# Counting the adjacency in groups of four chunks that share one PSUM bank

## The reference

```
x = x + relational layer(h): segment_sum of norm * (h @ weight[etype])[src] over dst
x = x + two gcn_conv layers(h): out = A_norm @ (h @ W) + b
x = x + equivariant message layer(h): messages of 128-node features, edge filters, segment_sum over src
x = x + two sage_conv layers(h): (segment_sum(x[src], dst) / deg) @ W_l.T + x @ W_r.T + b
```

## Time and profile before

| | us |
|---|---|
| median of 3 runs | 2048.51 |
| lowest, highest | 2046.33, 2052.84 |
| span of the profiled execution | 1473.0 |
| median less span | 575.5 |
| from the first to the last count | 209.3 |
| TensorE busy, share of the span | 93% |
| VectorE, ACT, POOL busy, share of the span | 59%, 34%, 60% |

### The profile page before, as it was taken

The page is one execution under the profiler, slowest core; times in us unless marked ns, Lnnn a source line. Parts: engine busy times, 40 slices in busy tenths (PEclk is TensorE's granted clock), DMA queues, the critical chain, the costliest instruction groups (busy, mean ns, idle before and its releaser), DMA issues.

```text
span 1473.0 us, 24743 instructions
## 1 busy us (share of the span) xinstructions
PE 1374.9 (93%) x6924; PEld 931.9 (63%) x6925; DVE 868.2 (59%) x2488; ACT 494.3 (34%) x1269; POOL 886.3 (60%) x930
## 2 busy tenths in 40 slices
PE   4887899999999999999999978999999979999998
PEld 1787788888884433344694855666666646686565
DVE  8777655555555768766423337888888854411111
ACT  7000000000006887773511225555555536311100
POOL 5777777777777777777777757777777720000000
PEclk9999899999999999999999988999999979999999
DMA  4688789888885552224101123222222210000001
GB/s 162 194 232 234 237 285 306 254 246 264 264 259 153 152 155 77 76 78 136 26 25 26 31 78 104 65 70 69 66 73 66 73 22 1 29 1 28 8 29 36
DMA packets 103451, 172.67 MB, mean 117 GB/s; under 512 B 20076, under 2 KB 53409, under 8 KB 103361
## 3 DMA queue, kind: packets, MB, share of 16 engines
q0 software_dynamic: 42832, 103.15, 23.8%
q10 hardware_dynamic: 26560, 38.90, 8.6%
q1 hardware_dynamic: 33968, 29.47, 6.5%
HBM read 153.74 MB, written 17.70 MB: 116 GB/s over the span
## 4 chain that ended last, share of the span: by engine, by line
PE 38%; POOL 28%; issue 19%; DMA 11%; DVE 2%; SPq 1%; POOLq 1%; ACT 1%; DVEq 0%; ACTq 0%
PE ps L983 15%; POOL slots L868 15%; POOL u L905 12%; PE ps L1065 5%; PE ps L1005 4%; DMA gath<-h_rows,idx 4%; PE ps L1077 3%; PE ps L1090 3%; DMA slots<-att,idx_s 3%; PE ps L1284 2%; PE ps L1272 2%; DMA u<-u_rows,at 2%; DMA att<-in_attr_dram 2%; POOL gath L842 1%; DVE et L1446 0%
## 5 line engine op out<-in xcount | busy, mean ns | idle before, releaser
L868 POOL DMA_INDIRECT slots<-att,idx_s x313 | 313.8, 1003 | 107.2 <-issue 95.4
L842 POOL DMA_INDIRECT gath<-h_rows,idx x313 | 302.8, 967 | 95.4 <-issue 71.0
L983 PEld LDWEIGHTS ps<-spread,gath 128*128 128x128 f32 x2504 | 307.9, 198 | 73.1 <-issue 41.4
L983 PE MATMUL ps<-spread,gath 128*128 128x96 f32 x2504 | 311.9, 281 | 26.4 <-DMA gath<-h_rows,idx 12.6
L1005 PE MATMUL ps<-base_t,z 128*128 128x512 f32 (+1 forms) x640 | 322.0, 614 | 0.0
L905 POOL DMA_INDIRECT u<-u_rows,at x243 | 239.3, 985 | 83.0 <-issue 70.7
L1512 DVE TENSOR_TENSOR z<-z,ps 128x384 f32 x313 | 172.9, 552 | 103.5 <-PE ps L983 94.7
L1206 PE MATMUL ps<-msg,hot 128*128 128x256 f32 x648 | 161.2, 392 | 22.3 <-DVE msg L1923 21.0
L1206 PEld LDWEIGHTS ps<-msg,hot 128*128 128x128 f32 x648 | 117.4, 190 | 84.4 <-DVE msg L1923 66.2
L599 ACT ACTIVATE z<-ps 128x512 f32<-128x512 f32 x5 | 3.0, 597 | 409.4 <-PE ps L1005 409.3
L1689 DVE TENSOR_TENSOR cnt<-cnt,ps 128x120 f32 x313 | 88.4, 282 | 62.9 <-PE ps L1297 49.5
(11 more groups left out here) (286 smaller groups left out, 1864.6 us busy)
## 6 DMA issues: line engine op xcount, KB each, us to landing
base_t<-in_bases_dram ACTq DMA_DIRECT2D x116, 256.0 KB
slots<-att SPq DMA_DIRECT2D x21, 256.0 KB, 5.0
at<-slots SPq DMA_DIRECT2D x21, 256.0 KB, 2.6
att<-in_attr_dram SPq DMA_DIRECT2D x79, 64.0 KB
gath<-h_rows,idx POOLq DMA_INDIRECT x313, 4.3
slots<-att,idx_s POOLq DMA_INDIRECT x313
u<-u_rows,at POOLq DMA_INDIRECT x243, 2.5
z<-in_x_dram SPq DMA_DIRECT2D x9, 256.0 KB, 5.5
```

The costliest lines, as they stand in the source:

```text
L842: nc.gpsimd.indirect_dma_start(out=gath[:, c % RING, :], out_offset=None, in_=h_rows, in_offset=bass.IndirectOffsetOnAxis(ap=idx[:, par, c ...
L868: nc.gpsimd.indirect_dma_start(out=slots, out_offset=bass.IndirectOffsetOnAxis(ap=idx_s[0:r, turn_of, c:c + 1], axis=0), in_=att[0:r, par, ...
L983: last = mm(bank[:, k * SPREAD:(k + 1) * SPREAD], gath[:, h_slot, k * P:(k + 1) * P], s_of.rearrange("p b d -> p (b d)"), start=True, stop ...
```

## The change

A group is now four chunks. TensorE writes their counts to four ranges of 120 columns of one PSUM bank, bank 5 and bank 7 in turn by group. It waits once for each group (hot_ok, hot_src, and a_add for the group two before) and signals `a_pe` once, with the last count of the group; chunk 313 is a group of its own and stands right behind the last group of four. `counted` is rounded down to whole groups, so that four counts stand together behind one product, and two or three products between them. VectorE waits for the group's signal, makes the four `hot_d` of the next group in a row with one signal, and then adds the four chunks in a row; each add still waits for the one before. ACT's pairs wait for the group in which their ring slot was last read.

```diff
--- before.py
+++ after.py
@@ -348,7 +348,8 @@
 
         def counted(i):
 
-            return max(0, min(REAL_CHUNKS, (i + 1 - COUNT_FROM) * REAL_CHUNKS // COUNTED))
+            there = max(0, min(REAL_CHUNKS, (i + 1 - COUNT_FROM) * REAL_CHUNKS // COUNTED))
+            return there if there == REAL_CHUNKS else there // QUAD * QUAD
 
         def due(c):
 
@@ -602,7 +603,7 @@
             def source_pair(p):
 
                 if p >= PAIRS:
-                    act.wait_ge(a_pe, 2 * (p - PAIRS) + 2)
+                    act.wait_ge(a_pe, (p - PAIRS) // 2 + 1)
                 for c in range(2):
                     last = nc.scalar.activation(hot_s[:, p % PAIRS, c, :], iota_a[:, 0:P], ACT.Abs,
                                                 bias=src_neg[:, 2 * p + c:2 * p + c + 1])
@@ -642,7 +643,7 @@
                     act.dma_start(x_high[m - HALF][0:LAST, :], x[m * P:m * P + LAST, :]).then_inc(ld_xh, 16)
                     for k in range(2, KIN):
                         act.dma_start(w1_t[k], g_w1[k * P:(k + 1) * P, :]).then_inc(ld_w1, 16)
-                while pairs <= REAL_CHUNKS // 2 and 2 * (pairs - PAIRS) + 2 <= counted(tile_end(t - KIN + 1) - 1):
+                while pairs <= REAL_CHUNKS // 2 and ((pairs - PAIRS) // 2 + 1) * QUAD <= counted(tile_end(t - KIN + 1) - 1):
                     source_pair(pairs)
                     pairs += 1
             assert pairs == REAL_CHUNKS // 2 + 1
@@ -1287,15 +1288,18 @@
 
             def count(t):
 
-                pe.wait_ge(hot_ok, t + 1)
-                if t % 2 == 0:
-                    pe.wait_ge(hot_src, t // 2 + 1)
-                if t == 0:
-                    pe.wait_ge(o_free, 2)
-                if t >= 2:
-                    pe.wait_ge(a_add, t)
-                mm(ps[5 + t % 2 * 2][:, 0:AWIN], hot_s[:, t // 2 % PAIRS, t % 2, :], hot_d[:, t % QUAD, 0:AWIN], start=True, stop=True)\
-                    .then_inc(a_pe, 1)
+                g, q = t // QUAD, t % QUAD
+                if q == 0:
+                    pe.wait_ge(hot_ok, g + 1)
+                    pe.wait_ge(hot_src, min(2 * g + 2, REAL_CHUNKS // 2 + 1))
+                    if g == 0:
+                        pe.wait_ge(o_free, 2)
+                    if g >= 2:
+                        pe.wait_ge(a_add, (g - 1) * QUAD + 1)
+                last = mm(ps[5 + g % 2 * 2][:, q * AWIN:(q + 1) * AWIN], hot_s[:, t // 2 % PAIRS, t % 2, :],
+                          hot_d[:, q, 0:AWIN], start=True, stop=True)
+                if q == QUAD - 1 or t == REAL_CHUNKS - 1:
+                    last.then_inc(a_pe, 1)
 
             def degrees():
 
@@ -1675,21 +1679,24 @@
                 all_ranks()
             v.memset(cnt_f[:, CLEARED:], 0.0).then_inc(dve_o, n_v.up())
 
-            def make_hot(t, slot):
-                v.tensor_scalar(hot_d[:, slot, 0:AWIN], iota_a[:, 0:AWIN], acol[:, bass.ds(t, 1)], None, ALU.is_equal)\
-                    .then_inc(hot_ok, 1)
-
-            def count_oct(g, further=OCT, chunks=OCT):
+            def make_hot(t):
+                return v.tensor_scalar(hot_d[:, t % QUAD, 0:AWIN], iota_a[:, 0:AWIN], acol[:, bass.ds(t, 1)], None, ALU.is_equal)
+
+            def count_oct(g, chunks=OCT):
                 w = load4(win_i[0:1, bass.ds(g * OCT, OCT)], DSTP - WIN)
                 for q in range(chunks):
                     t = g * OCT + q
-                    dve.wait_ge(a_pe, t + 1)
+                    if q % QUAD == 0:
+                        dve.wait_ge(a_pe, t // QUAD + 1)
+                        further = range(t + QUAD, min(t + 2 * QUAD, REAL_CHUNKS))
+                        for n in further:
+                            last = make_hot(n)
+                        if further:
+                            last.then_inc(hot_ok, 1)
                     dve.wait_ge(a_add, t + 1)
                     cw = cnt[:, :, bass.ds(w[q], WIN)]
-                    v.tensor_tensor(cw, cw, ps[5 + q % 2 * 2][:, 0:AWIN].rearrange("p (d s) -> p s d", s=BLOCKS), ALU.add)\
-                        .then_inc(a_add, 1)
-                    if q < further:
-                        make_hot(t + QUAD, q % QUAD)
+                    v.tensor_tensor(cw, cw, ps[5 + t // QUAD % 2 * 2][:, q % QUAD * AWIN:(q % QUAD + 1) * AWIN]
+                                    .rearrange("p (d s) -> p s d", s=BLOCKS), ALU.add).then_inc(a_add, 1)
                     low, apart = divmod(t - LOW_OCT * OCT, LOW_APART)
                     if apart == 0 and 0 <= low < 3 * HALF:
                         take_low(low // 3, low % 3)
@@ -2010,14 +2017,14 @@
             with dve.If(fit == 1):
                 v.tensor_scalar(src_neg, srclo[:, :], -1.0, None, ALU.mult).then_inc(src_ok, 1)
                 for t in range(QUAD):
-                    make_hot(t, t)
+                    last = make_hot(t)
+                last.then_inc(hot_ok, 1)
                 dve.wait_ge(cnt_zero, 1)
                 dve.wait_ge(dve_o, shared_waits)
                 v.memset(turn[:, 1:2], 0.0).then_inc(a_add, 1)
-                for g in range(OCTS - 1):
+                for g in range(OCTS):
                     count_oct(g)
-                count_oct(OCTS - 1, QUAD + 1)
-                count_oct(OCTS, 0, 1)
+                count_oct(OCTS, 1)
                 dve.wait_ge(a_add, REAL_CHUNKS + 1)
                 sum_blocks()
                 layers(adj, True)
```

## The result

| | median, us | runs |
|---|---|---|
| kernel before, same chip | 2048.8 (2032.5 to 2081.6) | 20 |
| changed kernel | 2039.6 (2016.3 to 2064.8) | 20 |

The ratio is 0.9945, with a 95% interval from 0.9919 to 0.9971. That is 9 us by the medians and 11 us by the ratio, which leaves out the executions of the slower state; the interval reaches from 6 to 17 us. The prediction said 18.3 us slower, 2067 us, and a range from 2052 to 2080 us.

A forecast was written before the change was run, and what follows sets the result against it. It took POOL's scatters to bound the kernel before and VectorE to pace the changed count stage: 20.4 us later, less 2.1 us of room, is +18.3 on 2048.5 us, 2067 us; range 2052 to 2080 us.

The forecast's parts named there:

- What lies outside the span: Whole execution: 575.5 us of the 2048.5 us median lie outside the profiled span of 1473.0 us and stay unchanged.
- VectorE's pace: Count stage: VectorE needs 2.95 us a group, 227.1 us in all, more than PE's 2.50, so it sets the pace.
- three further adds: VectorE, each group: adds in a row wait for one another and stand 0.48 us apart, 1.44 us for three.
- last make_hot to first add: VectorE, each group: from the start of the fourth make_hot to the first add, 0.25 us taken, 0.22 to 0.28.
- The load of positions: VectorE, once in two groups: loading eight window positions behind an add costs 0.50 us more, 19.0 us over 38 loads.
- The takes: VectorE, count stage: fifteen additions for the rows above stand between adds and cost 0.32 us each, 4.8 us.
- PE's term: PE, count stage: fewer changes between products and counts, and fewer waits, could shorten its stage by 7.6 to 15 us.
- One of the signs that the prediction had named against itself: PE, count stage: the prediction is wrong if PE isn't kept waiting by hot_d; 0.5 to 1 us before most short-gap groups expected.
- The meeting point: Before the first u gather: scatters' branch comes last, PE's has 2.1 us of room; PE's gain is lost, further loss seen.
- Rival 1: VectorE, count stage: adds in a row 0.28 us apart, PE the bound, scatters hide its gain; same time, 2048.5 us; chance 0.13.
- Rival 2: Before the first u gather: PE's branch is last, so its 7.6 to 15 us are real; 2034 to 2041 us; chance 0.03.
- Rival 3 (the clock): PE, count stage: waits at most groups lower its clock, 40% of groups lost at 1.2 GHz; +11 us, 2078 us; chance 0.06.

The follow-up runs named there:

- late_after: Changed kernel with POOL's scatters held until VectorE begins to sum the counts, chip A (before takes 1473 to 1477 us): 1682.3 us.
- a_here: Changed kernel without further edit, on a chip where the kernel before takes 1473 to 1477 us: 1471.9 us, ratio 0.9983 to before.
- lean: Changed kernel with every base product but the first of each block on 256 of its 512 columns, chip A: time within 0.2% of before.
- two_waits: Changed kernel with a second, already met wait (on a ScalarE semaphore) in front of each add, chip A: ratio 0.9984 to before.
- sig4_again: Changed kernel with a signal on each of the 313 counts again, chip B (before takes 2049 to 2073 us): ratio 0.993 to before.
- between_again: Changed kernel with eight places for destination hots and each make_hot between two adds as before, chip B: ratio 0.9927 to before.
- deep: Changed kernel with eight places for both destination and source hots, so two whole groups in flight, chip B: ratio 0.9916 to before.
- late_before: Kernel before with POOL's scatters held until VectorE begins to sum the counts, chip A: 1691.4 us.

## Why the prediction was wrong

**What lies outside the span.** "575.5 us of the 2048.5 us median lie outside the span, which I leave as they are." This failed first. In every run on record the span lies about 2 us under its own execution's time; a span and a time 28% apart were of two behaviours, and every term read from the trace holds for the one that was not timed. It did not by itself turn the sign: where the signals come at once, the change isn't slower either (0.9983).

**The term that was mis-sized.** This is the step that turned the sign: VectorE's pace, 2.95 us for a group and 227.1 us for the stage, which made VectorE and not PE the bound. Measured, the stage is 197.1 us (late_after, a_here), 2.53 for a group, and with PE's work cut down 191.5 us, 2.45 for a group (lean). The two parts of the difference, for each group:
- "three further adds: 3 x 0.48 = 1.44": they are 0.41 apart, 0.21 us less. The 0.48 of the earlier trace rows was read from adds with two waits, and put down to the dependence between them. The two_waits run puts the wait back and gets 0.48. The row was right; what it was taken to be was wrong.
- "last make_hot to first add", 0.25 on top of 0.66: the four hots and the way to the add are 0.65 together, 0.26 less. In a row they follow 0.16 us apart ((0.73 - 0.25)/3), not 0.22, which came from a row with a stretched make_hot in it.

Together 0.47 x 78 = 37 us, and 227.1 - 37 = 190, beside the 191.5 of lean, of which a part is still waits. The load of positions was sized right: in lean 1.32 us from the last add of a group to the next add with a load (580.03 to 581.35), 0.83 without, so 0.49 against 0.50 taken. The takes cost 0.38 instead of 0.32.

**PE's term.** 7.6 to 15 us were forecast for PE alone and 12.5 came, and 2.50 us for a group stand against 2.53 measured. So the term was right, and PE is the bound, but in the sum the term above hid it. One of the signs that the prediction had named against itself came: on a chip A, PE is hardly kept waiting by hot_d (0.3 us of idle time in 190).

**The meeting point.** "1.2 to 2.8 us of room" for PE's branch: in two further executions on chips A it had none. The frame was right there: 12.5 us on PE's branch brought 2.5, and leaving out 143 products brought nothing. On a chip B it doesn't hold at all. There the last scatter is issued 346 us before the first gather, and what PE's branch gains behind the scatters is seen in full.

**Where the 9 us come from on a chip B.** While the scatters run (437 to 443 us there, 422 to 428 on chips A), neither kernel gets far: 115 counts in before and 108 in the changed one, which is no faster there (3.7 and 3.9 us a count). The rest goes at nearly the pace of a chip A. Before: 198 counts from 979.0 to 1113.5, 0.683 us each, begun 4 us after the last scatter. Changed: 205 from 962.4 to 1096.1, 0.655 each, begun within 1 us. The difference of 0.028 is worth 5.5 us over 198 counts. Taken from the last scatter's end, before needs 0.70 us for each count that is left; changed, sig4_again, between_again and deep need 0.64 to 0.66. That makes 9 to 11 us over some 200 counts, against 9.2 measured (11 by the ratio). On a chip A without scatters beside them it was 9.1. This is an account and not a proof. There is one trace of before from a chip B, the traces are from different chips, and the number of counts that are left differs by more (197 in sig4_again, 253 in deep) than the effect is large.

**The rivals.** Rival 1's mechanism (adds in a row cost less apart) was half right, 0.41 and not 0.28, and its outcome is what chips A show. Rival 2 had PE's branch last and an outcome of 2034 to 2041 us. The measured 2039.6 lies in it, for its reason (the branch is last and gains what PE gains), but by luck as to the rest: it supposed a near tie, and PE's branch was last by more than 300 us. It had 0.03. Rival 3 (the clock) did not show: in the undisturbed stage the clock is 1.00. Beside the scatters on chips B it falls, in before as well (0.53, and 0.58 in the changed kernel, from 560 to 960 us), with PE busy for 120 and 100 of these 400 us. So the fall isn't the change's.

The prediction set a rule of the Trainium skill ("VectorE: DVE Perf Modes", section "The DRAIN you can't avoid") against the row, and gave the row the last word. The rule says that a semaphore after each operation costs nothing extra. For signals the traces agree: four make_hots last 0.72 us with a signal after each (late_before, 450.80) and 0.72 with one for the four (late_after, 451.44). It doesn't say what a wait costs, nor whether its copies waited for one another, so it neither bears out nor denies the 0.41. In these runs one more met wait costs 0.07 us on an add.

## What to carry over

- Compare the span with the times before anything else. If they are more than a few us apart, the trace may be of other conditions than the times, and the sum has to be made for both.
- A start-to-start distance in a row belongs to that instruction with its waits. Before it is used for a changed program, count the semaphores that each instance waits for, and look whether one of the instances was stretched by another engine.
- Where one signal serves a group and there is only one group's worth of buffers, the work placed between groups must be at least as long as the ring (signal, new buffers, first use). Here rounding the placement made 0.655 us a count out of what was 0.89 without it.

## What the runs showed of the hardware

- The same program (before, unchanged) takes 1473 to 1477 or 2049 to 2073 us. Chips 7, 10, 12 and 14 showed the first, 0, 2 and 4 the second. That it goes by the chip isn't shown beyond doubt. Only chip 12 was measured twice (the first both times), and in order of time the measurements came as two of kind A, three of kind B and three of kind A, within 49 minutes. The first comparison, of kind B, came before them; its chip's number isn't on record.
- On kind B, what waits for a TensorE signal starts up to 26 us behind the end of its record in the changed kernel while GpSimd's indirect scatters run. In the same stage without them the stage takes 196.7 us, as on kind A. The scatters themselves hardly slow down: 437 to 443 us on B, 422 to 428 on A. The edge stage with its indirect gathers suffers less than the counts: 488 to 497 us from the first gather to the first scatter, instead of 402 to 406.
- What the rate goes by is open. It isn't the number of updates (sig4_again), nor what is in flight (deep). Beside the scatters the kernels get through one count and its one or two products in 3.6 to 4.5 us, deep in 5.2. The ends of matmuls are modelled in the trace, so whether TensorE itself is slow or only its updates no run here tells; the two kernels made for it ran on the other kind.
- One more semaphore wait, already met, in front of a VectorE operation that depends on the one before: 0.48 instead of 0.41 us from start to start.
- VectorE's make_hots last 269 ns in the mean and up to 499 beside GpSimd's scatters, 246 ns and at most 251 with GpSimd idle (before and late_before, chips A). In the changed kernel this costs nothing: its stage is 197.1 us with and without scatters.
- On TensorE the change from 512-column products to the counts and back costs 0.05 to 0.06 us in the stream, however many counts stand together; each further count costs 0.054 us.
